# Six pairs' key projections of the second cross attention moved into the first attention's loop

## The reference, cut to what matters

```python
q = query @ w_q
kv = context @ w_kv
k, v = jnp.split(kv, 2, axis=-1)
# 16 heads of 64, q/k/v split into them
scores = jnp.einsum('bhqd,bhkd->bhqk', q, k) * SCALE
attn = jax.nn.softmax(scores, axis=-1)
out = jnp.einsum('bhqk,bhkd->bhqd', attn, v)
return out @ w_out + b_out
```

## Time and profile before

| | us |
|---|---|
| runs (median of 3) | 557.04 |
| lowest, highest | 556.35, 563.35 |
| the profiled execution's own time | 562.62 |
| its span in the trace | 560.8 |
| TensorE busy with products | 487.8 (87%) |
| VectorE, ScalarE, GpSimd busy | 283.2, 221.0, 101.5 |

### The profile page before, as it was taken

The page is one execution under the profiler, slowest core; times in us unless marked ns, Lnnn a source line. Parts: engine busy times, 40 slices in busy tenths (PEclk is TensorE's granted clock), DMA queues, the critical chain, the costliest instruction groups (busy, mean ns, idle before and its releaser), DMA issues.

```text
span 560.8 us, 11515 instructions
## 1 busy us (share of the span) xinstructions
PE 487.8 (87%) x4512; PEld 347.0 (62%) x4512; DVE 283.2 (50%) x662; ACT 221.0 (39%) x359; POOL 101.5 (18%) x143
## 2 busy tenths in 40 slices
PE   8669988887689986789985899999998999999994
PEld 3456666664538953345563677777787667777774
DVE  2954566616764253334435966666614343333336
ACT  1324566641313300125432566666650643333330
POOL 2820112443100031000005222222221000000001
PEclk9865899998869998569997999999999999999998
DMA  7786430040400005700010000001000011111110
GB/s 202 254 289 212 137 107 2 3 152 0 151 0 1 1 1 213 255 6 3 2 40 12 12 13 13 13 21 28 2 1 1 20 28 39 38 38 38 38 28 37
DMA packets 23897, 34.36 MB, mean 61 GB/s; under 512 B 6400, under 2 KB 14544, under 8 KB 23600
## 3 DMA queue, kind: packets, MB, share of 16 engines
q1 hardware_dynamic: 23856, 33.77, 18.7%
HBM read 26.95 MB, written 6.82 MB: 60 GB/s over the span
## 4 chain that ended last, share of the span: by engine, by line
PE 71%; DVE 18%; ACT 4%; DMA 2%; issue 2%; POOL 1%; SPq 0%; POOLq 0%; DVEq 0%; ACTq 0%
PE ps L1024 10%; PE ps L1007 10%; PE ps L923 5%; DVE negm L1318 5%; PE ps L622 4%; PE ps L633 3%; PE ps L673 3%; PE ps L646 3%; PE ps L896 3%; PE ps L685 3%; PE ps L995 3%; PE ps L649 2%; PE ps L904 2%; PE ps L607 2%; PE ps L912 2%
## 5 line engine op out<-in xcount | busy, mean ns | idle before, releaser
L1318 DVE TENSOR_REDUCE negm<-ps 128x8 f32<-128x1024 f32 x48 | 56.5, 1219 | 55.1 <-PE ps L633 55.1
L1650 DVE SCALAR_TENSOR_TENSOR racc<-ps,sm,racc 128x128 f32<-128x128 f32 x128 | 35.9, 344 | 63.2 <-PE ps L1024 63.1
L1072 ACT ACTIVATE arena<-ps,w1a 128x512 f32<-128x512 f32 x64 | 43.4, 687 | 59.0 <-PE ps L1007 57.8
L1072 ACT ACTIVATE probs<-ps 128x1024 f32<-128x1024 f32 (+2 forms) x52 | 48.9, 989 | 39.7 <-PE ps L649 39.3
L1024 PEld LDWEIGHTS ps<-w1a,arena 128*128 128x128 f32 x512 | 59.4, 192 | 7.2 <-issue 6.2
L1024 PE MATMUL ps<-w1a,arena 128*128 128x128 f32 x512 | 59.8, 275 | 0.8 <-DVE racc L1641 0.8
L1007 PE MATMUL ps<-xT,w1a 128*128 128x512 f32 x128 | 58.0, 594 | 1.4 <-ACT xT L1072 1.4
L1072 ACT ACTIVATE arena<-ps 128x512 f32<-128x512 f32 (+4 forms) x62 | 35.1, 574 | 43.1 <-PE ps L831 15.8
L586 POOL TENSOR_TENSOR probs<-probs,rzE 128x480 f32<-128x480 f32 x32 | 30.6, 987 | 76.0 <-DVE rzE L1588 76.0
L545 POOL TENSOR_SCALAR rstd<-mv 128x4 f32<-128x4 f32 x12 | 2.7, 227 | 223.1 <-DVE mv L1379 223.1
L607 PE MATMUL ps<-onesb 128*128 128x512 bf16 x134 | 38.5, 424 | 3.0 <-DVE sm L1510 2.1
(11 more groups left out here) (191 smaller groups left out, 836.3 us busy)
## 6 DMA issues: line engine op xcount, KB each, us to landing
stacks<-arena SPq DMA_DIRECT2D x12, 512.0 KB, 3.7
near<-stacks SPq DMA_DIRECT2D x12, 256.0 KB, 3.5
near<-stacks SPq DMA_DIRECT2D x24, 128.0 KB, 3.4
late<-stacks SPq DMA_DIRECT2D x12, 256.0 KB, 3.6
late<-stacks SPq DMA_DIRECT2D x24, 128.0 KB, 3.5
w1a<-in_w1a SPq DMA_DIRECT2D x1, 2048.0 KB, 7.5
w2a<-in_w2a SPq DMA_DIRECT2D x1, 2048.0 KB, 7.6
w1a<-in_w1b SPq DMA_DIRECT2D x16, 128.0 KB, 2.0
```

The lines of the kernel that those rows point to most:

```text
L1072: return nc.scalar.activation(o, i, f, **kw)
L1318: nc.vector.tensor_reduce(negm[:, n % 2, 8 * h:8 * h + 8], pair_of(a.use, "s", n, h), AX.X, ALU.max, negate=True).then_inc(a.max, 1)
L1650: last = stt(racc[:, b, :], bank(banks + half)[:, k * P:(k + 1) * P], sm[:, 11, bass.ds(b * E1 + e, 1)], racc[:, b, :], ALU.mult, ALU.add)
```

## The change

- TensorE: the two fillers in A's `head_values` go. A new `keys_ahead(n, pair, half)` stands at the end of steps 2 to 13 of A's loop, behind the second part of the values: one product of 96 x 128 by 96 x 480 into BANK_M for half a pair's keys, pairs 0 to 5 in order. It waits for the new weights (once), for the copy of the maxima of head n + 1 and for the division two heads back.
- TensorE: `head_token` in A waits in addition until ScalarE has copied the keys of the step before (`ka_copied`).
- ScalarE: at the end of those steps it copies the 128 x 480 keys out of BANK_M, behind `outT`, into `kA` (pairs 0 to 3, in the arena where the rotary keys lay, hence the one wait for `A.kept`), `kB` (three halves, new) and `wqk0` (the last half).
- SyncE: one load of all of E's key weights, `wkA` (96 x 1024, 384 KB), on its queue behind the second half's first key piece and before the stacks of heads 4 to 7. The loads for each pair stay, those of its key weights too.
- Pair loop: `project_keys` and its two copies go for pairs 0 to 5. Values of those pairs wait for the copies of their queries instead, and for nothing at pair 0; scores wait for the queries' copies of their half, and for keys only at pairs 6 and 7.
- The hardware loops of the pair loop on TensorE and ScalarE are unrolled; VectorE, GpSimd and SyncE keep theirs.
- `selT` moves over `sel` in the arena. The semaphore `ld_p` is gone (the pick table counts with `ld_l`, whose waits are now for 7 loads), and the waits for `ld_d` are for 11 loads.

```diff
-        selT = area(4096, E0, T, dt=BF16)
+        selT = area(0, E0, T, dt=BF16)
...
+        kA = area(4 * T, 4, B * L)
+        kB = sb("kB", [P, 3, B * L // 2])
+        wkA = area(8 * T, NH * XD, rows=CD)
...
             keep_keys(1, 0)
+            load(wkA, d["wkE"], ld_d)
             heads(A, 4, 4, NH)
...
-                    if a is A:
-                        keep_busy(2, BANK_V)
...
                 pe.wait_ge(a.mc, min(n + 3, count))
+                if a is A and n + 2 > FIRST_KEYS:
+                    pe.wait_ge(ka_copied, min(n + 2 - FIRST_KEYS, 2 * AHEAD_KEYS))
...
+            def keys_ahead(n, pair, half):
+
+                if pair == 0 and half == 0:
+                    pe.wait_ge(ld_d, 16 * 11)
+                pe.wait_ge(A.mc, n + 2)
+                pe.wait_ge(A.div, n - 1)
+                mm(bank(BANK_M)[:, 0:480], wkA[:, pair * P:(pair + 1) * P], ctxT[:, half * 480:(half + 1) * 480],
+                   start=True, stop=True).then_inc(ka_made, 1)
...
                         head_values(a, n - 1, 1)
+                    if a is A and 0 <= n - FIRST_KEYS < 2 * AHEAD_KEYS:
+                        keys_ahead(n, *divmod(n - FIRST_KEYS, 2))
...
             def project_values(n, slot):
                 for half in range(2):
-                    pe.wait_ge(e_kc, n * 2 + half + 1)
+                    if n >= AHEAD_KEYS:
+                        pe.wait_ge(e_kc, (n - AHEAD_KEYS) * 2 + half + 1)
+                    elif n > 0:
+                        queries_copied(n, half)
...
-                pe.wait_ge(e_kc, n * 2 + (2 if g >= 2 else 1))
+                queries_copied(n, g // 2)
+                if n >= AHEAD_KEYS:
+                    pe.wait_ge(e_kc, (n - AHEAD_KEYS) * 2 + g // 2 + 1)
...
-                    project_keys(n + 1, 1 - slot)
+                    if n + 1 >= AHEAD_KEYS:
+                        project_keys(n + 1, 1 - slot)
...
-            project_keys(0, 0)
             project_values(0, 0)
...
-            pair_step(0, 0, 1)
-            pair_step(1, 1, 1)
-            with pe.Fori(1, PAIRS // 2 - 1) as i:
-                for u in range(2):
-                    pair_step(i * 2 + u, u, i + 1)
-            pair_step(PAIRS - 2, 0, PAIRS // 2)
-            pair_step(PAIRS - 1, 1, PAIRS // 2, last=True)
+            for n in range(PAIRS):
+                pair_step(n, n % 2, n // 2 + 1, last=n == PAIRS - 1)
...
                         copy_outputs(n - 1)
+                    if a is A and 0 <= n - FIRST_KEYS < 2 * AHEAD_KEYS:
+                        i = n - FIRST_KEYS
+                        if i == 0:
+                            act.wait_ge(A.kept, 16 * 8)
+                        act.wait_ge(ka_made, i + 1)
+                        fn(keys_E(i // 2, i % 2), bank(BANK_M)[:, 0:480], ACT.Copy
+                           ).then_inc(ka_copied, 1)
```

More of the change, by code:

```diff
@@ L46 @@
 LOADS = 3
+AHEAD_KEYS = 6
+FIRST_KEYS = 2
 BIG = -1e30
@@ L216, in decoder_kernel, with keys_E @@
         kE = area(12288, 2, B * L)
+        kA = area(4 * T, 4, B * L)
+        kB = sb("kB", [P, 3, B * L // 2])
+        wkA = area(8 * T, NH * XD, rows=CD)
+        def keys_E(n, half):
+            cols = slice(half * 480, (half + 1) * 480)
+            if n < 4:
+                return kA[:, n, cols]
+            if n < AHEAD_KEYS:
+                at = 2 * (n - 4) + half
+                return kB[:, at] if at < 3 else wqk0[:].rearrange("p a b -> p (a b)")[:, 0:480]
+            return kE[:, n - AHEAD_KEYS, cols]
         wE = area(14208, 2, 3, P)
@@ L276, in decoder_kernel @@
         dchain, achain, pchain = sem("dchain"), sem("achain"), sem("pchain")
-        ld_p = sem("ld_p")
+        ka_made, ka_copied = sem("ka_made"), sem("ka_copied")
         stack = [sem(f"stack{k}") for k in range(RING)]
@@ L285, in __init__ @@
                 self.qk = sem(n + "_qk")
-                self.mul = sem(n + "_mul")
+                self.mul = sem(n + "_mul") if turns == 0 else None
                 self.full = sem(n + "_full")
@@ L356, in _ @@
             load(wproj0[:], d["wproj0"], ld_l)
-            load(pick_in, d["con"][:, C_PICK:C_HOST], ld_p)
+            load(pick_in, d["con"][:, C_PICK:C_HOST], ld_l)
             load(con[:, C_IOTA:C_ALL], d["con"][:, C_IOTA:C_ALL], ld_r)
@@ L567, in _ @@
             rsqrt(2, 1)
-            pool.wait_ge(ld_d, 16 * 10)
+            pool.wait_ge(ld_d, 16 * 11)
             add_bias(3, boD)
@@ L897, in project_queries, with queries_copied @@
                        start=True, stop=True).then_inc(e_q, 1)
+            def queries_copied(n, half):
+                pe.wait_ge(e_qa, n * 2 + half + 1)
+                pe.wait_ge(e_qd, n * 2 + half + 1)
             def project_keys(n, slot):
                 for half in range(2):
-                    if not early(n, 1):
-                        pe.wait_ge(e_qa, n * 2 + half + 1)
-                        pe.wait_ge(e_qd, n * 2 + half + 1)
+                    queries_copied(n, half)
                     mm(bank(BANK_M0 + half)[:, 0:480], wE[0:CD, slot, 1, :], ctxT[:, half * 480:(half + 1) * 480],
@@ L923, in pair_scores @@
                     last = mm(bank(BANK_S + g % 2)[:, k * L:(k + 1) * L], qz[:, slot, b, j, :],
-                              kE[:, slot, b * L:(b + 1) * L], start=True, stop=True)
+                              keys_E(n, b // 4)[:, b % 4 * L:(b % 4 + 1) * L], start=True, stop=True)
                 last.then_inc(e_s, 1)
@@ L1133, in _ @@
             fn(lams[:, 2:4], lams[:, 0:2], ACT.Exp).then_inc(lam_exp, 1)
-            act.wait_ge(ld_p, 16)
+            act.wait_ge(ld_l, 16 * 7)
             fn(pick[:], pick_in, ACT.Copy).then_inc(tables, 1)
@@ L1212, in copy_keys_values @@
             def copy_keys_values(n, slot):
-                for half in range(2):
-                    act.wait_ge(e_k, n * 2 + half + 1)
-                    fn(kE[:, slot, half * 480:(half + 1) * 480], bank(BANK_M0 + half)[:, 0:480], ACT.Copy).then_inc(e_kc, 1)
+                for half in range(2 if n >= AHEAD_KEYS else 0):
+                    act.wait_ge(e_k, (n - AHEAD_KEYS) * 2 + half + 1)
+                    fn(keys_E(n, half), bank(BANK_M0 + half)[:, 0:480], ACT.Copy).then_inc(e_kc, 1)
                 for half in range(2):
@@ L1265, in _ @@
                 pair_exps(0, 0, g)
[L1266 to L1272, removed]
+            for n in range(PAIRS):
+                pair_step(n, n % 2, last=n == PAIRS - 1)
             table_of(ACT.Gelu)
@@ L1423, in _ @@
             high_piece(A, 1)
-            dve.wait_ge(ld_l, 16 * 6)
+            dve.wait_ge(ld_l, 16 * 7)
             link(tt(lamin[:, 0:2, :], lamin[:, 0:2, :], lamin[:, 2:4, :], ALU.mult))
@@ L1535, in _ @@
             ln_apply(2, 1)
-            dve.wait_ge(ld_d, 16 * 10)
+            dve.wait_ge(ld_d, 16 * 11)
             for n in range(2):
```

## The result

The changed kernel takes 594.15 us (median of 4, 591.83 to 596.79), the kernel before 557.42 (4 runs): a ratio of 1.0645, with a 95% interval of 1.0562 to 1.0728. It was forecast at 546.6, in a range of 542 to 553. It is slower by 37 us where 10 fewer were expected.

What follows compares the result with a forecast made beforehand. TensorE was taken to bound both loops, at full clock nearly everywhere. Gains of 7.6 us in the pair loop and 2.8 in the first attention, 10.4 together, took 557.04 to 546.6 us, range 542 to 553.

Steps and rivals of the forecast that it cites:

- Rival (c): First attention: clock falls for want of fillers, 3.4 us more per key step, 583 us with ten; chance 0.05.
- (a): First attention: clock rises 6 to 8 us sooner through large key products, 3 to 4 us more gained, 543; chance 0.13.
- the third attention reached full clock: Reason given against a clock loss in the first attention: the third attention's stretch in the trace reached full clock; no size.
- 3 us either way for the clock: Allowance for the clock's rise shifting either way with work of another shape: 3 us.
- Part 1: Pair loop: keys leave it, 1.78 us less in each of four steps, 7.6 in all, bounds 6.4 and 8.1.
- Pair 1's step: Pair loop, step preparing pair 1: VectorE's sums hold the first maximum, so only 0.45 us gained, bounds 0 and 0.50.
- Part 2: First attention: fillers leave; one pair costs 0.43 us where TensorE is the bound, sixteen pairs.
- Part 3: First attention: keys enter at 0.80 to 0.90 us each; step 4.50 against 4.66, bounds 4.37 and 4.80.
- The -0.4 for the first steps: First attention, steps at half clock: fillers go, key products come, about 0.4 us less, bounds -2 and +1.5.
- The added wait on the key copy: First attention: the token's transposes wait for ScalarE's key copy, done in time with a margin of 0.2 us.
- The wait for the bank: First attention: scores need a bank freed by ScalarE's first exponential; it just fits, margin 0.04 us.
- The rest: Key weights' load, unrolled loops, masks' address and semaphore changes: priced at nothing, bounds 0 and 1 for load and unrolling.

Runs made afterwards that it cites:

- no_fillers: The kernel before without its sixteen pairs of fillers in the first attention, nothing else changed: 584.37 us, ratio 1.043.
- keys_and_fillers: The changed kernel with its two fillers back in front of the first part of the values, keys kept: 558.69 us, ratio 1.000.
- padded_keys: The changed kernel, no fillers, with context and key weights padded to 128 rows by 32 rows of zeros: 554.98 us, ratio 0.993.
- fillers_first_steps: The changed kernel with fillers only in the first attention's steps for the values of heads 0 to 3: 554.54 us, ratio 0.989.
- keys_twice: The changed kernel with each key product issued twice, no fillers: 615.08 us, ratio 1.098.
- fillers_at_keys: The changed kernel with two fillers directly ahead of each key product, none elsewhere: 556.69 us, ratio 0.997.

## Why the prediction was wrong, point by point

- **Where it ended up.** Rival (c) is what happened, at a chance of 0.05: for want of fillers the clock didn't fall but never came. Its price, 583 with ten steps at 3.4 us more, was short: the step is 8.33 against 4.66, 3.67 more, and the stretch went on behind the last key product, to near 155 us.
- **The step that failed** is the one that set the chances: "the keys bring more array time than the fillers did", against (c) and for (a). True, and it doesn't matter: twice the keys left the clock at 0.50, 32 rows of zeros brought it up. The text had seen that being busy is not all that it takes, and then weighed the filler by its time only. I called a key product "a large tile like the filler (96x128 against 128x128)"; those 32 rows are what made the difference. The other reason against (c), that the third attention reached full clock, was a misreading too. Its loop has no filler ahead of the values, but its mask products (L622) have the fillers' own form, as its rows before show:

```profile
256.80 0.81 PE L622 MATMUL ps<-causT,identb 128*128 128x512 bf16 x3
...
259.85 1.02 PE L622 MATMUL ps<-causS,identb 128*128 128x512 bf16 x4
```

- **The rule that I weighed.** The Trainium skill (TensorE: Matmul & The Clock Gate, "What's actually happening") has busy-ness release the clock. I said that the rows disagree, and still let the sum stand by it: only 3 us either way for the clock. no_fillers measures what the rule hides: 4.3%, some 24 us, for sixteen pairs of fillers of 0.43 each.
- **Part 1, the pair loop: right.** Steps of 12.01 against 13.86 give 1.85 where 1.78 was taken (bounds 1.60 and 1.90). Pair 1's step was to gain 0.45. From the first queries to the second step's it is 24.08 before and 23.64 in keys_and_fillers and in padded_keys, 0.44 less, and again 22.29 against 21.85 with the full clock in both. VectorE's sums held it as said: in the trace after, its first maximum of that step starts at 359.16, directly behind them. In the changed kernel itself this stretch took 24.92, since the clock there was at 0.50 until near 350 us (the stretches of the trace after):

```profile
338.00:342.00 4.00, 1.11 (x4) 0.71 (x4) 2.47 (x4) 0.32 (x1) 2.27 (x2) 0.50 0.00 0
342.00:346.00 4.00, 3.67 (x4) 1.17 (x4) 0.69 (x1) 0.87 (x2) 2.34 (x1) 0.50 0.00 0
346.00:350.00 4.00, 3.17 (x15) 3.09 (x15) 1.65 (x3) 0.59 (x1) 0.00 (x0) 0.50 0.14 41
```

  In the earlier trace rows one slice there is a 7, and the queries' first 3.79 us were at half clock before too; after, the scores behind them were as well. Summed, the pair loop's stage is 7.5 shorter in padded_keys; 7.6 was forecast. The step that prepares pair 7 took 13.96 there, 0.1 more than before.
- **Part 2, the fillers' own price: right, and beside the point.** 5.07 in keys_and_fillers less 4.75 in fillers_first_steps is 0.32 where TensorE had a little wait left; in the direct order 0.43.
- **Part 3, the keys' price: too low.** 1.00 us for 0.80 to 0.90, so a step of 4.75 and not 4.50, within the bounds of 4.37 and 4.80 (the lower one is below what its own terms add up to, 4.44). The -0.4 for the first steps isn't the sum of its terms either: -0.45 and +0.85, less at most the 0.53 of the wait, give -0.1 to +0.4. At full clock keys in place of fillers cost 0.09 a step and save nothing. That is 2.5 us over ten steps. The added wait on the key copy never showed: in no kernel did the token's transposes wait for it. The wait for the bank did, by 0.04 to 0.05 a step, as the margin of 0.04 had let fear.
- **The rest, right.** The load of all key weights delayed no stack: the stages ahead of the loop are no longer than before, and the step's chain has no transfer in it. The unrolled loops show no time.
- **What the change would have brought** with the clock held, as one knows from padded_keys: 554.98, a ratio of 0.993. Of the profiled executions its span is 8.4 shorter: 7.5 in the pair loop and 2.1 elsewhere, less 1.1 lost in the first attention's stage, where 2.8 less was forecast. Over the runs less is left of it; both kernels vary by 7 us and more, which I take to be the moment at which the clock comes. When it comes was seen in the profiled runs alone, but the mean granted clock goes with the time: in the runs of the kernel before, 0.928 to 0.934 at 555.8 to 559.8 us, 0.916 to 0.926 at 560.3 to 563.8.

## What to carry to other kernels

An instruction whose result nobody reads can be the most valuable in its loop: before removing a filler, ask what the clock did in the stretch before it, and what other work of the same shape is there to take its place. Replace it only by products that use as many rows and columns (fewer rows failed here; fewer columns than 480 of the moving operand, or than 128 of the weights, were not tried); where the work has fewer rows, pad the operands with rows of zeros, which cost no time here. And where the trace shows TensorE busy all the time at half clock, price the whole loop at both levels, with a real chance for each: here 12 steps at 3.67 us stood against a gain of 10.

## What the runs showed of the hardware

- TensorE, busy for 80 us on end (60 to 140 in the trace after), stayed at 1.2 GHz while its work was small tiles (32 rows or 32 columns) and transposes with products of 96 rows among them, be these 1.90 of 8.33 us or 3.50 of 9.93, in float32 or bf16.
- The same loop came to 2.4 GHz when those products had 128 rows, in either type and with the last 32 rows all zeros. With 96-row products, or with none, the clock came only in the last steps, where the new scores are gone (0.83 at 170 to 171 us in keys_twice, TensorE busy throughout). When it comes differs between runs: near 63 us with the padded keys, near 86 us in one run with 480 columns of the identity.
- A loop can keep a level that it doesn't reach by itself: with 96-row keys alone behind the first fillers the clock stayed full to the loop's end (fillers_first_steps). Of twelve runs with no keys there, five took 11 us or more longer than the longest of the rest, and the one of them that was profiled had lost it.
- At full clock two fillers take 0.54 us behind the 32-column values and 0.43 behind the token's transposes; a key product takes 1.00 behind the values and 0.81 behind fillers (fillers_at_keys).
